# A two-layer transformer block on one core: norming, weight loads and a weight split moved from a stage's start into the stage before it

## The chip, the cores and the metric

The kernel runs on one core of a Trainium2 chip. The metric is the device time of one execution in microseconds (us). A core has TensorE (matrix products, with a queue of weight loads beside it), VectorE, ScalarE, GpSimd, and SyncE, which here only issues transfers. In rows they are PE, PEld, DVE, ACT, POOL and SP. Each engine runs its own instructions in order and waits for the others by semaphores.

## What is computed

A sequence of 2048 tokens of width 512 goes through four sublayers, each followed by a layernorm of the sum with its input. This case touches the seam between the first two.

```python
# differential attention: 16 head pairs, HD = 16, causal
aw = softmax(q @ k.T * HD**-0.5 + causal)                  # two maps per pair
aw = aw[:, :, 0] - lam * aw[:, :, 1]
attn = aw @ v                                              # 32 values per head
attn = attn * rsqrt(mean(attn * attn, -1) + 1e-5) * (1 - LAMBDA_INIT)   # norm per head
x = layernorm(x + attn @ Wo)
# mixture of experts: 8 experts, top 2, plus a low-rank part
scores = softmax(x @ G);  w = the two largest, kept
out = sum over e of w_e * (silu(x @ gate_e) * (x @ up_e)) @ down_e  +  low-rank (lora_A, lora_B)
x = layernorm(x + out)
# then a state-space layer (Mamba 2) and an int8 feed-forward
```

## The kernel before, in words

Tokens lie on the 128 partitions, in 16 tiles of 128 (`TT`). The program is a chain of blocks, each ended by a barrier of all engines: `qkv`, `attention`, `attend_out`, `experts`, `scan`, `finish`. Products are exact to float32: each operand is split in a high part (rounded, on ScalarE) and a low part (the rest, by subtraction, on VectorE or GpSimd), and `product3` adds three products. So each weight matrix is loaded raw, then split, before TensorE can use it.

**Attention** loops over 16 head pairs. A pair has 40 units (`units`): query chunk c of 512 tokens, key tile j of 128. Chunk 0 is units 0 to 3, chunk 1 is 4 to 11, chunk 2 is 12 to 23, chunk 3 is 24 to 39. For each unit TensorE writes scores (L440), ScalarE takes Exp of 2 x 512 of them (L510), and TensorE multiplies by V (L460). On the diagonal (the last four units of a chunk, 512, 384, 256 and 128 columns wide) GpSimd first zeroes the upper triangle (L368). TensorE writes the scores of unit u + 2 after Exp u and ahead of the product of unit u. When a chunk is full, ScalarE copies it (L537), TensorE turns it (L469), and VectorE's `combine` (L582 to L592) writes four tiles of `A`, one head's 32 columns. In all pairs but the last VectorE also reduces score maxima for later pairs; in the last it has only `combine`. Six times per pair, after units 15, 17, 26, 28, 30 and 32 (`SPLIT_AT`), ScalarE makes the high half of a later layer's weight (L517, L521), GpSimd the low half (L375), and SyncE stores both and loads the next.

**`attend_out`** has 21 slots, and in each every engine does steps for different tiles. The order is written by hand:
- TensorE in slot s: turn tile s of `A` (L718), turn tile s-3 of the result (L737), the router's and low-rank products of tile s-4 (`ao_pf`), the product with `Wo` of tile s-1 (`ao_po`).
- ScalarE: high part of `A` (`high_a`, L776), of the result (`high_x`, L780), a copy (L788), the root of a head norm (L770), squares (L766, 128x512), the layernorm's root (L784); behind slots 7, 11, 15 and 19 an Exp for four tiles' routing (L819).
- VectorE: scale tile s+1 of `A` by its head norms (L832, L834), low part `low_a` (L840), `low_x` (L844), sums of squares of tile s+2 (L825, L828), layernorm of tile s-2 (L864, L866), a copy (L870), then `add` of tile s-1: the sum with x (L854), its statistics (L856, L858) and variance (L860). Behind slots 7, 8, 11, 12 and so on come the routing steps of four tiles (L881 to L910).

SyncE loads `Wo`, `first` (low-rank and router weights), x, `gate`, and, when `Wo`'s raw copy is free, `up` in the same place. ScalarE and VectorE split `Wo` and `first`, ScalarE and GpSimd split `gate` (slot 0) and `up` (slot 2), 128x2048 each (L792, L708). The array `V_then_X` holds V in attention and the layer's result afterwards; the raw weights stand in its not yet written tiles.

## Time and profile before

| | us |
|---|---|
| median of three runs | 3621.58 (3617.08 to 3626.28) |
| the profiled execution | 3622.66 |
| its span | 3620.7 |
| TensorE busy | 3422.7 (95%) |
| VectorE busy | 2696.8 (74%) |
| ScalarE busy | 1947.7 (54%) |
| GpSimd busy | 918.3 (25%) |
| TensorE's granted clock, mean | 0.976 of full |

A row of a timeline has the start in us from the span's start, the duration, engine, line, operation, what is written from what, and in brackets how long the engine stood idle before it and what ended that. Lines are those of the kernel before. A row with x4 or x8 merges several instructions. The clock has two levels, 1.2 and 2.4 GHz. Attention ends at 1238 us, `attend_out` begins at 1239.1, `experts` at 1373.

### The profile page before, as it was taken

Reading aid. Unit: us, or ns where it says so; the run is one execution under the profiler, and the core shown is the slowest. Engines: PE = TensorE matmul, PEld = TensorE weight load, DVE = VectorE, ACT = ScalarE, POOL = GpSimd, SP = SyncE. Lnnn points to the kernel's source line nnn. Section 1 sums busy time; section 2 is a strip of 40 time slices with the busy share of each in tenths; the row PEclk is TensorE's granted clock in tenths of the full one; section 3 lists DMA queues with packets and bytes.
Section 4 is the critical chain, followed back from the end, with each engine's and each line's share of the span. In section 5 each row is a group of like instructions: output and inputs, shape, how many; then the busy total and the mean of one; then the engine's idle time right before and its main releaser. Section 6 shows DMA issues by size and latency. Waiting matters only on the chain. (4 is left out here: it accounts for less than half of the span.)

```text
span 3620.7 us, 58447 instructions
## 1 busy us (share of the span) xinstructions
PE 3422.7 (95%) x20912; PEld 2392.3 (66%) x20912; DVE 2696.8 (74%) x5252; ACT 1947.7 (54%) x2496; POOL 918.3 (25%) x821
## 2 busy tenths in 40 slices
PE   8889999999999788969999999999999999979998
PEld 6544444444444467756777777777777777758886
DVE  3577777777777384677999889998998889864444
ACT  3156656666667633434666566665666666543332
POOL 0022222222222200003443434443444444420000
PEclk9989999999999898989999999999999999989999
DMA  7443443443432211236555655565555555530100
GB/s 231 72 91 93 106 89 89 112 89 104 101 88 89 97 36 35 84 133 201 183 175 180 222 174 164 177 217 184 182 177 192 189 179 177 177 131 27 35 12 24
DMA packets 254975, 463.04 MB, mean 128 GB/s; under 512 B 48224, under 2 KB 62432, under 8 KB 251616
## 3 DMA queue, kind: packets, MB, share of 16 engines
q1 hardware_dynamic: 254688, 459.30, 41.6%
q8 instruction: 169, 2.77, 0.3%
q14 instruction: 118, 0.97, 0.1%
HBM read 363.49 MB, written 95.16 MB: 127 GB/s over the span
## 5 line engine op out<-in xcount | busy, mean ns | idle before, releaser
L510 ACT ACTIVATE probs<-prob_scores 128x1024 f32<-128x1024 f32 (+3 forms) x640 | 572.4, 896 | 381.0 <-PE prob_scores L440 373.1
L460 PE MATMUL times_v<-probs,VS 128*64 128x256 f32 (+2 forms) x4608 | 612.4, 382 | 14.2 <-ACT outT L537 13.0
L557 DVE TENSOR_REDUCE part_max<-ring 128x1 f32<-128x512 f32 x720 | 462.8, 685 | 115.3 <-PE ring L432 113.6
L49 PE MATMUL sc_pip<-sc_xh,sc_wl 128*128 128x512 f32 x1024 | 453.1, 443 | 18.6 <-DMA sc_xl<-x_low 14.0
L460 PEld LDWEIGHTS times_v<-probs,VS 128*64 128x64 f32 x4608 | 279.7, 136 | 253.7 <-issue 162.6
L1627 POOL TENSOR_TENSOR sc_xdd<-sc_xdt,sc_small 128x512 f32<-128x512 f32 x128 | 248.2, 1939 | 640.7 <-DVE sc_xdt L1849 640.7
L51 PE MATMUL sc_pip<-sc_xh,sc_wh 128*128 128x512 f32 x1024 | 405.8, 396 | 0.0
L50 PE MATMUL sc_pip<-sc_xl,sc_wh 128*128 128x512 f32 x1024 | 402.4, 393 | 0.0
L1840 DVE SCALAR_TENSOR_TENSOR sc_ca<-sc_xr,sc_chan,sc_ca 128x512 f32<-128x512 f32 x384 | 292.9, 763 | 13.6
L440 PE MATMUL prob_scores<-QS,KS 50*128 50x512 f32 (+3 forms) x1280 | 298.7, 463 | 1.6 <-ACT probs L510 1.6
L440 PEld LDWEIGHTS prob_scores<-QS,KS 50*128 50x128 f32 x1280 | 119.6, 184 | 214.2 <-ACT probs L510 121.0
L554 DVE CUSTOM_DVE_ANT_0 masked_scores<-ring,later_keys 128x128 f32<-128x128 f32 x480 | 216.2, 487 | 52.6 <-PE ring L432 49.5
L49 PEld LDWEIGHTS sc_pip<-sc_xh,sc_wl 128*128 128x128 f32 x1024 | 193.5, 189 | 91.2 <-issue 40.5
L432 PE MATMUL ring<-KS,QS 48*128 48x512 f32 (+3 forms) x1200 | 235.4, 388 | 12.8 <-DVE part_max L557 8.6
L1651 POOL TENSOR_TENSOR sc_ssq<-sc_ssq,sc_sq 128x512 f32<-128x512 f32 x112 | 181.1, 1617 | 252.2 <-ACT sc_sq L1802 252.2
L50 PEld LDWEIGHTS sc_pip<-sc_xl,sc_wh 128*128 128x128 f32 x1024 | 193.8, 189 | 69.4 <-issue 29.7
L1886 DVE TENSOR_TENSOR sc_gl<-sc_gx,sc_gh 128x512 fp32r<-128x512 f32 x128 | 223.2, 1744 | 0.0
L51 PEld LDWEIGHTS sc_pip<-sc_xh,sc_wh 128*128 128x128 f32 x1024 | 193.1, 189 | 42.1
L368 POOL TENSOR_SCALAR_AFFINE_SELECT probs<-probs 128x256 f32<-128x256 f32 x256 | 104.0, 406 | 456.8 <-ACT probs L510 456.8
L1691 PE MATMUL sc_py<-sc_M,sc_xdt 128*64 128x128 f32 x2048 | 207.4, 281 | 9.6 <-DVE sc_M L1860 9.6
L375 POOL TENSOR_TENSOR w_lo<-w_raw,w_hi 128x512 fp32r<-128x512 f32 x96 | 122.6, 1277 | 354.6 <-ACT w_hi L521 349.3
L49 PE MATMUL sc_pop<-sc_woh,sc_gl 128*128 128x512 f32 x512 | 204.9, 400 | 0.9 <-DVE sc_acc L1897 0.9
(333 smaller groups left out, 7215.2 us busy)
## 6 DMA issues: line engine op xcount, KB each, us to landing
sc_wh<-scan_W_high SPq DMA_DIRECT2D x256, 256.0 KB, 2.7
sc_wl<-scan_W_low SPq DMA_DIRECT2D x256, 256.0 KB, 3.0
sc_ce<-scan_expa SPq DMA_DIRECT2D x128, 512.0 KB, 5.2
sc_woh<-scan_Wo_high SPq DMA_DIRECT2D x128, 256.0 KB, 4.0
sc_wol<-scan_Wo_low SPq DMA_DIRECT2D x128, 256.0 KB, 4.6
w_raw<-in_Wg SPq DMA_DIRECT2D x64, 256.0 KB, 2.8
scan_W_high<-w_hi SPq DMA_DIRECT2D x64, 256.0 KB, 2.0
scan_W_low<-w_lo SPq DMA_DIRECT2D x64, 256.0 KB, 2.3
```

The source lines that it names most:

```text
L49: pe.matmul(out, ll, rh, start=start, stop=False)
L50: pe.matmul(out, lh, rl, start=False, stop=False)
L51: return pe.matmul(out, lh, rh, start=False, stop=stop)
L432: pe.matmul(slot(place["max", q, t, s])[:, 0:w], QS[q % NQK][rows, i * P:(i + 1) * P], KS[q % NQK][rows, c * CHUNK:c * CHUNK + w], start=T ...
L440: mm = pe.matmul(pb[u % 2][:, s, 0:w], KS[b][rows, j * P:(j + 1) * P], QS[b][rows, (c + 1) * CHUNK - w:(c + 1) * CHUNK], start=True, stop= ...
L460: mm = pe.matmul(po[MV * s:MV * (s + 1), CHUNK - w + n * h:CHUNK - w + (n + 1) * h], VS[p % 2][:, j, :], PT[u % NPT][:, s, n * h:(n + 1) * ...
L510: act.activation(PT[u % NPT][:, :, 0:w], pb[u % 2][:, :, 0:w], ACT.Exp).then_inc(exped, 1)
L554: dve.tensor_tensor_reduce(out=masked_out[:, s, 0:w], in0=slot(n)[:, 0:w], in1=later[:, CHUNK - w:], scale=1.0, scalar=NEG, op0=ALU.add, o ...
L557: dve.tensor_reduce(to, slot(n)[:, 0:w], AX.X, ALU.max).then_inc(emptied, 1)
L1627: pool.tensor_tensor(xdd[t % 2][:, :, :], xdt[t % 2][:, :, :], bc(t, 1), ALU.mult).then_inc(xdd_made, 1)
L1840: dve.scalar_tensor_tensor(out=to, in0=src, scalar=w, in1=to, op0=ALU.mult, op1=ALU.add).then_inc(conv if last else conv_step, 1)
L1886: dve.tensor_tensor(gl[t % 2][:, :, :], gx[:, :, :], gh[t % 2][:, :, :].bitcast(F32), ALU.subtract).then_inc(g_low, 1)
```

## The change

Three things move from `attend_out` into the last pair of attention.

1. The raw weights `Wo`, `first`, `up` and `gate` (3.4 MB) are loaded by SyncE once the last pair's V is staged, ahead of that pair's stores. `gate` and `up` have places of their own now, so the second load into `Wo`'s place falls away. `attend_out` waits for none of them.
2. `up` is split in the last pair in four pieces of 128x512: high halves on ScalarE behind Exp 19 to 22, the first waiting for all loads, low halves on GpSimd behind the four weight splits that follow unit 23's triangle.
3. Tiles 0 to 11 of `A` are squared and summed by VectorE behind the `combine` of chunks 0, 1 and 2, two tiles an operation; one step makes the mean squares of 12 tiles, ScalarE takes their root in one Sqrt behind unit 28's weight split, and VectorE takes the reciprocal and scales 12 tiles ahead of its last `combine`. `attend_out` squares, sums and scales only tiles 12 to 15 (`LATE`).

The array of mean squares is the same for both stages (`inv_rms`, before `ao_ms`).

```diff
@@ attention
+    UP_AT, ROOT_AT = (19, 20, 21, 22), 28
+    up_hi, up_lo = g.QS[1], g.KS[1]
+    NORMED = 4 * (NCH - 1)
@@ GpSimd, behind the low halves that follow a unit's triangle
+                        if p == PAIRS - 1 and u == ends[NCH - 2]:
+                            for n in range(len(UP_AT)):
+                                pool.wait_ge(up_high, n + 1)
+                                pool.tensor_tensor(up_lo[:, piece(n)], g.raw_up[:, piece(n)], up_hi[:, piece(n)].bitcast(F32), ALU.subtract).then_inc(up_low, 1)
@@ SyncE, ahead of the last pair's stores
+                sp.wait_ge(v_staged, PAIRS)
+                for to, src in next_w:
+                    sp.dma_start(to, src).then_inc(next_in, 16)
                 keep_weights(PAIRS - 1)
+                sp.wait_ge(next_in, 16 * len(next_w))
@@ ScalarE, behind exp and split_high of unit n
+                        if n // NU == PAIRS - 1 and n % NU in UP_AT:
+                            k = UP_AT.index(n % NU)
+                            if k == 0:
+                                act.wait_ge(next_in, 16 * len(next_w))
+                                act.wait_ge(scored, (PAIRS - 1) * NU)
+                            act.activation(up_hi[:, piece(k)], g.raw_up[:, piece(k)], ACT.Copy).then_inc(up_high, 1)
+                        if n == (PAIRS - 1) * NU + ROOT_AT:
+                            act.wait_ge(rms_ready, 1)
+                            act.activation(g.ms[:, 0:NORMED, :], g.ms[:, 0:NORMED, :], ACT.Sqrt).then_inc(rms_root, 1)
@@ VectorE
+                def sums(c):
+                    dve.wait_ge(out_done, (PAIRS - 1) * NCH + c + 1)
+                    for i in (4 * c, 4 * c + 2):
+                        if i:
+                            dve.wait_ge(summed, i // 2)
+                        rows = g.A[:, i:i + 2, :]
+                        dve.tensor_tensor(masked_out[:, :, :], rows, rows, ALU.mult).then_inc(squared, 1)
+                        dve.wait_ge(squared, i // 2 + 1)
+                        dve.tensor_reduce(g.ms[:, i:i + 2, :], masked_out[:, :, :].rearrange("p i (h d) -> p i h d", d=VD), AX.X, ALU.add).then_inc(summed, 1)
+                def scale_heads():
+                    c = 1.0 - LAMBDA_INIT
+                    ms = g.ms[:, 0:NORMED, :]
+                    dve.wait_ge(summed, NORMED // 2)
+                    dve.tensor_scalar(ms, ms, 1.0 / VD / c / c, LN_EPS / c / c, ALU.mult, ALU.add).then_inc(rms_ready, 1)
+                    dve.wait_ge(rms_root, 1)
+                    dve.reciprocal(ms, ms).then_inc(rms_inv, 1)
+                    dve.wait_ge(rms_inv, 1)
+                    for i in range(NORMED):
+                        rows = g.A[:, i, :].rearrange("p (h d) -> p h d", d=VD)
+                        dve.tensor_tensor(rows, rows, g.ms[:, i, :].unsqueeze(2).to_broadcast([P, PAIRS, VD]), ALU.mult).then_inc(scaled, 1)
@@ VectorE's loop
                         if u - 1 in ends:
                             combine(p, ends.index(u - 1))
+                            if p == PAIRS - 1:
+                                sums(ends.index(u - 1))
+                scale_heads()
                 combine(PAIRS - 1, NCH - 1)
@@ attend_out
+    LATE = TT - 4
@@ TensorE, turn_a
-                    pe.wait_ge(scaled, i + 1)
+                    if i >= LATE:
+                        pe.wait_ge(scaled, i - LATE + 1)
@@ ScalarE, ahead of the slots
-                square(0)
-                rms(0)
-                square(1)
-                weights_high(0, wo[0][:, :, :], raw_o)
-                rms(1)
-                square(2)
-                weights_high(1, wf[0][:, :, :], raw_f)
+                weights_high(wo[0][:, :, :], raw_o)
+                weights_high(wf[0][:, :, :], raw_f)
@@ VectorE
-                sums(0)
-                scale(0)
-                sums(1)
                 weights_low(0, wo[1][:, :, :], raw_o, wo[0][:, :, :])
                 for s in range(SLOTS):
-                    if s + 1 < TT:
+                    if LATE <= s + 1 < TT:
                         scale(s + 1)
@@
-                    if s + 2 < TT:
+                    if LATE <= s + 2 < TT:
                         sums(s + 2)
```

ScalarE in the last pair, from the copy of chunk 2 (`outT`) on. Before:

```order
L537 ACTIVATE outT<-times_v 128x512
L510 ACTIVATE probs<-prob_scores 128x1024
L517 ACTIVATE w_raw<-w_raw,w_norm 128x512
L521 ACTIVATE w_hi<-w_raw 128x512
L510 ACTIVATE probs<-prob_scores 128x1024 x2
L517 ACTIVATE w_raw<-w_raw,w_norm 128x512
L521 ACTIVATE w_hi<-w_raw 128x512
L510 ACTIVATE probs<-prob_scores 128x1024 x2
```

The same place now:

```order
L565 ACTIVATE outT<-times_v 128x512
L528 ACTIVATE probs<-prob_scores 128x1024
L535 ACTIVATE w_raw<-w_raw,w_norm 128x512
L539 ACTIVATE w_hi<-w_raw 128x512
L528 ACTIVATE probs<-prob_scores 128x1024 x2
L535 ACTIVATE w_raw<-w_raw,w_norm 128x512
L539 ACTIVATE w_hi<-w_raw 128x512
L560 ACT_TABLE_LOAD
L560 ACTIVATE inv_rms<-inv_rms 128x192
L528 ACT_TABLE_LOAD
L528 ACTIVATE probs<-prob_scores 128x1024 x2
```

Behind unit 28's split stand a table load, the Sqrt of 12 tiles' mean squares, and a second table load, ahead of Exp 29.

GpSimd at the end of attention, from the triangles of chunk 2 on. Before:

```order
L368 AFFINE_SELECT probs<-probs 128x2x128 x4
L375 TENSOR_TENSOR w_lo<-w_raw,w_hi 128x512 x4
L368 AFFINE_SELECT probs<-probs 128x2x128 x4
L346 UNCONDITIONAL_BRANCH
L2292 ISA
```

And now (`KS` is where `up`'s low half goes):

```order
L377 AFFINE_SELECT probs<-probs 128x2x128 x4
L384 TENSOR_TENSOR w_lo<-w_raw,w_hi 128x512 x4
L388 TENSOR_TENSOR KS<-V_then_X,QS 128x512 x4
L377 AFFINE_SELECT probs<-probs 128x2x128 x4
L355 UNCONDITIONAL_BRANCH
L2329 ISA
```

The four low halves of `up` come between the last weight split and the triangles of units 36 to 39.

VectorE at the start of `attend_out`. Before:

```order
L825 TENSOR_REDUCE ao_ms<-masked_scores 128x16
L828 TENSOR_SCALAR ao_ms<-ao_ms 128x16
L832 RECIPROCAL ao_ms<-ao_ms 128x16
L834 TENSOR_TENSOR A<-A,ao_ms 128x512
L825 TENSOR_REDUCE ao_ms<-masked_scores 128x16
L828 TENSOR_SCALAR ao_ms<-ao_ms 128x16
L874 TENSOR_TENSOR ao_wo_low<-V_then_X,ao_wo_high 128x2048
L832 RECIPROCAL ao_ms<-ao_ms 128x16
L834 TENSOR_TENSOR A<-A,ao_ms 128x512
L840 TENSOR_TENSOR ao_al<-ao_pa,ao_ah 128x512
```

And now:

```order
L914 TENSOR_TENSOR ao_wo_low<-V_then_X,ao_wo_high 128x2048
L880 TENSOR_TENSOR ao_al<-ao_pa,ao_ah 128x512
L914 TENSOR_TENSOR ao_wf_low<-V_then_X,ao_wf_high 128x544
L880 TENSOR_TENSOR ao_al<-ao_pa,ao_ah 128x512
L894 TENSOR_TENSOR V_then_X<-ao_po,later_keys 128x512
```

The low half of `Wo` is the stage's first work on VectorE, and the low part of tile 0 (`ao_al`) follows it directly.

## Rows read from the trace of the kernel before

**Rows 1.** Busy time by stretch, `attend_out`: us, then engines' busy time, clock, DMA
```profile
core 0: us, PE busy (x) PEld busy (x) DVE busy (x) ACT busy (x) POOL busy (x), PEclk, DMA share, GB/s
...
1272.40:1293.80 21.40, 20.92 (x132) 17.74 (x130) 20.53 (x53) 8.32 (x24) 0.00 (x0) 1.00 0.18 50
```

**Rows 2.** DMA issues at the stage's start: size, us to landing
```profile
V_then_X<-in_Wo SPq DMA_DIRECT2D x1, 1024.0 KB, 5.5
```

**Rows 3.** Timeline of the stage's start: start us, us, engine, line; idle before
```profile
1244.67 1.91 ACT L792 ACTIVATE ao_wo_high<-V_then_X 128x2048 fp32r<-128x2048 f32 x1 [2.84 <-DMA V_then_X<-in_Wo]
...
1250.62 0.77 PE L49 MATMUL ao_po<-ao_wo_high,ao_al 128*128 128x512 f32 x1
...
1254.73 0.60 PE L718 MATMUL ao_pa<-ident,A 128*128 128x128 f32 x4
...
1255.61 2.88 DVE L828 TENSOR_SCALAR ao_ms<-ao_ms 128x16 f32<-128x16 f32 x1
...
1260.05 0.15 DVE L860 TENSOR_SCALAR ao_rx<-row_stats 128x1 f32<-128x1 f32 x1
```

**Rows 4.** Timeline of VectorE, one slot of the stage
```profile
1288.45 0.15 DVE L860 TENSOR_SCALAR ao_rx<-row_stats 128x1 f32<-128x1 f32 x1
...
1289.40 0.68 DVE L840 TENSOR_TENSOR ao_al<-ao_pa,ao_ah 128x512 fp32r<-128x512 f32 x1
...
1290.60 0.68 DVE L825 TENSOR_REDUCE ao_ms<-masked_scores 128x16 f32<-128x512 f32 x1
...
1291.40 0.16 DVE L864 RECIPROCAL ao_rx<-ao_rx 128x1 f32<-128x1 f32 x1
...
1293.79 0.15 DVE L860 TENSOR_SCALAR ao_rx<-row_stats 128x1 f32<-128x1 f32 x1
```

**Rows 5.** Timeline of VectorE, two adds in the stage's tail
```profile
1343.61 0.69 DVE L854 TENSOR_TENSOR V_then_X<-ao_po,ao_x 128x512 f32<-128x512 f32 x1 [1.83 <-PE ao_po L51]
...
1348.55 0.69 DVE L854 TENSOR_TENSOR V_then_X<-ao_po,later_keys 128x512 f32<-128x512 f32 x1 [0.34 <-PE ao_po L51]
```

**Rows 6.** Timeline of the stage: clock falls, table load, slots with routing
```profile
1261.15 1.11 PE L718 MATMUL ao_pa<-ident,A 128*128 128x128 f32 x4 [3.07 <-DVE A L834]
...
1270.91 0.66 PE L737 MATMUL ao_px<-ident,V_then_X 128*128 128x128 f32 x4 [2.11 <-DVE V_then_X L866]
...
1294.20 1.28 ACT L819 ACT_TABLE_LOAD   x1
...
1295.49 0.23 ACT L819 ACTIVATE ao_ex<-ao_ex 128x32 f32<-128x32 f32 x1
...
1308.03 1.11 PE L737 MATMUL ao_px<-ident,V_then_X 128*128 128x128 f32 x4 [1.99 <-DVE V_then_X L866]
...
1309.62 0.15 DVE L860 TENSOR_SCALAR ao_rx<-row_stats 128x1 f32<-128x1 f32 x1
...
1317.65 0.15 DVE L860 TENSOR_SCALAR ao_rx<-row_stats 128x1 f32<-128x1 f32 x1
```

**Rows 7.** Timeline of attention's last pair, units 26 to 36
```profile
1216.68 0.87 DVE L592 TENSOR_TENSOR A<-out 128x128 f32<-128x128 f32 x1
...
1219.79 1.92 ACT L510 ACTIVATE probs<-prob_scores 128x1024 f32<-128x1024 f32 x2
...
1221.38 0.50 PE L440 MATMUL prob_scores<-QS,KS 50*128 50x512 f32 x2
...
1227.08 1.26 POOL L375 TENSOR_TENSOR w_lo<-w_raw,w_hi 128x512 fp32r<-128x512 f32 x1 [2.75 <-ACT w_hi L521]
...
1231.05 0.41 POOL L368 TENSOR_SCALAR_AFFINE_SELECT probs<-probs 128x256 f32<-128x256 f32 x1 [2.70 <-ACT probs L510]
...
1232.55 1.08 PE L460 MATMUL times_v<-probs,VS 128*64 128x256 f32 x8
```

**Rows 8.** VectorE's groups by shape, whole run: xcount, busy us, mean ns
```profile
L1860 DVE TENSOR_TENSOR sc_M<-sc_M,sc_CB 128x1024 f32<-128x1024 f32 x128 | 156.5, 1223 | 1.1 <-ACT sc_M L1777 1.1
...
L1352 DVE RECIPROCAL A<-A 128x256 f32<-128x256 f32 x4 | 7.0, 1753 | 0.1
```

More of the change, by code:

```diff
@@ L235, in _, with attention @@
                                       g.KS[0][rows, c * CHUNK:c * CHUNK + w], start=True, stop=True).then_inc(filled, 1)
-def attention(nc, g, QD, KD, lams, scan_w):
+def attention(nc, g, QD, KD, lams, scan_w, next_w):
     PARTS = 3 * HD
@@ L331, in attention @@
         out_inv, out_weight, out_weighed, out_done = (g.sem("out_" + n) for n in ("inv", "weight", "weighed", "done"))
+        next_in, up_high, up_low = g.sem("next_weights_in"), g.sem("up_high"), g.sem("up_low")
+        squared, summed, rms_ready, rms_root, rms_inv, scaled = (
+            g.sem("at_" + n) for n in ("squared", "summed", "rms_ready", "rms_root", "rms_inv", "scaled"))
+        piece = lambda n: slice(n * CHUNK, (n + 1) * CHUNK)
         loads = lambda q: 16 * 12 * (q // NQK + (q % NQK > 1))
@@ L631, with attend_out @@
 AR = LR + EX
-def attend_out(nc, g, x_dram, A, X, xh, xl, lr, w, Wo, first, gate, up, mv):
+def attend_out(nc, g, x_dram, A, X, xh, xl, lr, w, raw, mv):
     SLOTS = TT + 5
+    LATE = TT - 4
+    raw_o, raw_f, raw_g = raw
     NB = TT // 4
@@ L661, in attend_out @@
         sem = lambda name: g.sem("ao_" + name)
-        w_in, w_high, w_low, w_rest = [sem(f"w_in{n}") for n in range(4)], sem("w_high"), sem("w_low"), sem("w_rest")
+        w_high, w_low, w_rest = sem("w_high"), sem("w_low"), sem("w_rest")
         x_in = [sem(f"x_in{b}") for b in range(2)]
@@ L687, in load_x @@
                     sp.dma_start(xin[i % 2][:, :], x_dram[i * P:(i + 1) * P, :]).then_inc(x_in[i % 2], 16)
-                sp.dma_start(raw_o, by_row(Wo)).then_inc(w_in[0], 16)
-                sp.dma_start(raw_f, by_row(first)).then_inc(w_in[1], 16)
-                for i in range(2):
-                    load_x(i)
-                sp.dma_start(raw_g, by_row(gate)).then_inc(w_in[2], 16)
-                sp.wait_ge(w_low, 1)
-                sp.dma_start(raw_o, by_row(up)).then_inc(w_in[3], 16)
-                for i in range(2, TT):
-                    sp.wait_ge(added, i - 1)
+                for i in range(TT):
+                    if i >= 2:
+                        sp.wait_ge(added, i - 1)
                     load_x(i)
@@ L705, in _ @@
                                    pattern=[[1, EX], [-1, EX]], channel_multiplier=0).then_inc(made, 1)
-                for n, (raw, (hi, lo)) in enumerate(((raw_g, wg), (raw_o, wu))):
-                    pool.wait_ge(w_high, 3 + n)
-                    pool.tensor_tensor(lo[:, :], flat(raw), hi[:, :].bitcast(F32), ALU.subtract).then_inc(w_rest, 1)
-                pool.wait_ge(w_rest, 2)
+                pool.wait_ge(w_high, 3)
+                pool.tensor_tensor(wg[1][:, :], flat(raw_g), wg[0][:, :].bitcast(F32), ALU.subtract).then_inc(w_rest, 1)
+                pool.wait_ge(w_rest, 1)
             @block.tensor
@@ L788, in keep_l, with weights_high @@
                     act.activation(lr[:, i, :], pf[i % 2][:, 0:LR], ACT.Copy).then_inc(read_l, 1)
[L790 to L791 removed]
+                def weights_high(hi, raw):
                     act.activation(hi, raw, ACT.Copy).then_inc(w_high, 1)
[L794 to L800 removed]
+                weights_high(wo[0][:, :, :], raw_o)
+                weights_high(wf[0][:, :, :], raw_f)
                 for s in range(SLOTS):
@@ L923, in _ @@
                         low_x(s - 3)
-                    if s + 2 < TT:
+                    if LATE <= s + 2 < TT:
                         sums(s + 2)
@@ L2329, in two_layers @@
                 qkv(nc, g, xT, Wq, Wk, Wv, QD, KD)
-            with nc.sbuf_tensor("A", [P, TT, E], F32) as g.A:
-                attention(nc, g, QD, KD, (lq1, lk1, lq2, lk2), (Wg, WoT, norm_table, D["W"], D["Wo"]))
+            with nc.sbuf_tensor("A", [P, TT, E], F32) as g.A, nc.sbuf_tensor("inv_rms", [P, TT, PAIRS], F32) as g.ms:
+                raw_f = X[:, 6:8, :].rearrange("p a n -> p (a n)")[:, 0:EK * AR].rearrange("p (k n) -> p k n", k=EK)
+                raw_o, raw_g, g.raw_up = X[:, 8:12, :], X[:, 2:6, :], X[:, 12:16, :].rearrange("p k n -> p (k n)")
+                attention(nc, g, QD, KD, (lq1, lk1, lq2, lk2), (Wg, WoT, norm_table, D["W"], D["Wo"]),
+                          ((raw_o, by_row(Wo)), (raw_f, by_row(first)), (X[:, 12:16, :], by_row(up)), (raw_g, by_row(gate))))
                 g.end_stage()
@@ L2336, in two_layers @@
                     lr = g.A[:, 0:4, :].rearrange("p a (b n) -> p (a b) n", n=LR)
-                    attend_out(nc, g, x, g.A, X, xh, xl, lr, w, Wo, first, gate, up, mv)
+                    attend_out(nc, g, x, g.A, X, xh, xl, lr, w, (raw_o, raw_f, raw_g), mv)
                     experts(nc, g, X, xh, xl, lr, w, g.A[:, 4:, :].rearrange("p a n -> p (a n)"), (down, lora_b, scan_first),
```

35 lines of the change are left out of this document (15 added, 20 removed).

## The prediction

> **What bounds the kernel now.** The edit touches two neighbouring places: attention's last pair (to 1238 us) and the stage behind it, `attend_out` (1239 to 1373 us). I read the windows of that stage first. In its even stretch [rows 1] TensorE is busy 20.9 of 21.4 us and VectorE 20.5: both are nearly full, so work taken from VectorE gives back only the distance to TensorE's own limit. Hence I followed one token tile from slot to slot. A tile's last row on VectorE is L860, the variance of its layernorm; from one L860 to the next is one slot, and the time table below is made of these rows. Then I read the stage's start, where everything waits for `Wo`'s transfer [rows 2, 3], and the last pair unit by unit, because the new waits and instructions go there.
>
> **The stage, slot by slot.** (a) *Start.* `Wo` takes 5.5 us from issue to landing [rows 2], and ScalarE splits it at 1244.67 [rows 3]. Now it is in place, so the split begins with the stage, at 1239.2: 5.5 earlier. VectorE's half starts 1.95 later and takes 2.29; `low_a(0)` comes right behind it, at 1243.3, with no reciprocal and scale of a tile between; the first product starts 0.9 later, 1244.2 against 1250.62. Before, the product took 4.1 (1250.62 to 1254.73, the transposes behind it), its first matmuls slow. I take 4.4, since TensorE rests ahead of it now. VectorE's add follows at 1248.7. Before, the add also stood behind L828, 2.88 us for 16 elements per row while GpSimd split 128x2048 [rows 3]; no L828 comes before tile 12 now. From the add to L860 it is 1.66 (0.71, 0.73 and 0.22 from start to start): tile 0 at 1250.3 against 1260.05, 9.7 earlier.
>
> (b) *One even slot* takes 5.34 before (1288.45 to 1293.79 [rows 4]). The sums (L825, L828) go, and L864 starts where L825 did: 0.80 less. The scale (L832, L834) goes too, but brings nothing: `low_a` (L840) starts 0.95 after L860, and the other way to it, ScalarE's root and `high_a`, takes as long. The scale only covered a wait. VectorE's chain becomes 4.54. TensorE's own slot is longer: in the stage's tail, where VectorE waits for it, its products end 4.94 apart [rows 5]. So an even slot becomes 4.94, a gain of 0.40, not the 1.7 of the removed work. In the first slots tiles of later steps are missing: 4.54 without `low_x` and the copy is 3.9, without the copy 4.45, and tile 3 meets TensorE, 4.75. Tiles 1 to 3: 1254.2, 1258.6, 1263.4. Three times 4.94: tile 6 at 1278.2, before 1293.79.
>
> (c) *Slots with routing.* Tiles 6 to 8 took 15.83 before (1293.79 to 1309.62 [rows 4, 6]): an Exp with its table load (1.28), then the routing steps. VectorE's chain sets these slots, and from it go the sums twice (1.60) and, behind the routing, one scale that hid nothing (0.89): 13.34 are left, tile 8 is at 1291.5, 18.1 earlier.
>
> (d) *The clock behind the routing.* Before, TensorE waited for a scale and then 1.99 for a norm, fell to 1.2 GHz (the 4 transposes at 1308.03 take 1.11), and tile 9 came 8.03 after tile 8 [rows 6]. Now one wait is left, for tile 7's norm, of 2.25 by the same table. An idle of 2.11 left the clock up at 1270.91, one of 3.07 had it down at 1261.15 [rows 6]; 2.25 is nearer to the first. Then tile 9 follows after 5.34 (it has sums again: tiles 12 to 15 are still normed here), 2.7 less. From there on nothing differs. **The stage ends 18.1 + 2.7 = 20.8 us earlier**; if the clock falls, 18.1.
>
> **What the last pair pays.** (e) *Four high halves of `up`* on ScalarE, 0.6 each (1.91 for 128x2048 [rows 3]), after units 19 to 22. Units 21 to 23 have 384, 256 and 128 columns of scores per half, so ScalarE, late by one piece at most, catches up: 0. The transfers (3.4 MB) are issued at the pair's start, some 25 us before they are wanted; end to end at 5.5 per MB [rows 2] they need 18.7: 0. Squares and sums of chunks 0 and 1 lie in VectorE's idle time: 0.
>
> (f) *The root at unit 28.* ScalarE is free for it at 1219.79, where Exp 29 starts before [rows 7]. VectorE ends `combine` of chunk 2 at 1217.55 (L592), and only then squares and sums tiles 8 to 11: two products of 128x1024 at 1.22 [rows 8] and two reductions of the same count, for which 0.68 at 512 [rows 4] gives 1.21: 4 x 1.25 = 5.0. The product reads two operands in SBUF, as L592 does, and L592 took 0.87 for 128 elements beside a split on GpSimd; one product meets such a split: 1.1 at most. With L828's successor, 0.3, the mean squares are ready at 1224.0 (1222.9 without the meeting). Sqrt 0.35, then the table load back to Exp, 1.28 [rows 6] (the load for Sqrt lies inside the wait): Exp 29 starts at 1225.7, **5.9 late**. Queued behind the root are Exp 29 to 39 and two weight splits; TensorE's scores of unit 31 (1221.38 [rows 7]) wait for Exp 29, with 0.6 of slack: 5.3 late. TensorE idles over 5 us by then, so as at 1261.15 it goes on at 1.2 GHz. Such a fall cost 2.7 at tile 9 and 1.2 in the stage's first product; I take 2.0. Unit 36's product, 1232.55 before, could start at 1239.8.
>
> (g) *Four low halves on GpSimd* stand behind its last weight split and ahead of the four triangular selects of units 36 to 39. That split was at 1227.08 [rows 7] and is now some 5.7 late, 1232.8. Five operations of 1.25 end at 1239.0, plus 0.6 to 1.2 for meeting VectorE's 12 scales, plus the select, 0.41 (1231.05 [rows 7]): unit 36 can start at 1240.3, half a us behind (f). So (f) and (g) nearly hide each other; alone, (g) would cost 1.1. VectorE's reciprocal of 192 (1.35, between 1.75 at 256 [rows 8] and the small ones) and 12 scales at 0.6 end by 1236, before its last `combine`: 0. **The last pair ends 8 us later**, between 5.5 (early mean squares, short fall of the clock) and 10.
>
> **The sum.** -20.8 + 8.0 = -12.8. The profiled execution took 3622.66 (span 3620.7), the median of three runs 3621.58. So 3609.9 on its own time and **3608.8** on the median, 0.35% faster.
>
> On the meeting of VectorE and GpSimd: the Trainium skill (SBUF — State Buffer, Who interferes with whom) says that a VectorE operation with two SBUF inputs and a GpSimd one that reads SBUF exclude each other for a whole instruction, whoever comes first. The trace agrees (L592, 0.87). By that rule the 12 scales in a row could hold GpSimd off longer than (g) has it, by another 1.2 or so.
>
> **Rivals.**
> *No stall at the root.* If the mean squares were there in time, the pair would pay two loads and the root (2.9 less 0.6) and little of (g): +2.5, sum -18.3, **3603.3**. Against it: the sums can't begin before 1217.55 and need 5 us, where ScalarE leaves 2.2. 0.14.
> *The stage gives less.* The clock falls at tile 9 (2.7), and GpSimd's split of `gate`, wanted at 1244.0, gets ahead of VectorE's `ao_wf_low`, wanted at 1243.9, and holds it 4.6 us, of which 1.3 reach the chain: sum -8.8, **3612.8**. Both are close calls. 0.25.
> *A table switch costs more than its load.* In the trace an Exp starts 0.01 behind its load's end (1294.20, 1.28, 1295.49 [rows 6]), which speaks against it; if each of the two added switches cost its load twice, 2.6: **3611.4**. 0.05.
> The Trainium skill (ScalarE: Activation LUTs, What ACT_TABLE_LOAD costs) gives a drain of 1.38 us with each switch; an estimate by it is this same rival.
> *Slower: the raw weights come late.* ScalarE's first high half, behind Exp 19, waits for all four transfers, and Exp 20 to 39 stand behind it. Each us beyond the 25 adds one. To lose over 11 us in all they must come 24 us late, that is take near 50 us where I bound them by 18.7: 3634. 0.03.
> *That the change doesn't do what it says*: the order of instructions shows all its parts; no chance kept.
>
> **How the numbers follow.** Forecast 0.53 (3605.5 to 3613), rivals 0.14, 0.25, 0.05, 0.03. A measurement of this kernel can tell about 0.3% (10.9 us) from no change; the line is 3610.7. Of the forecast's 0.53 some 0.42 lies below it, with the stall-free rival: faster 0.56. Same: 0.11 + 0.25 + 0.05 = 0.41. Slower: 0.03. Range 3602 to 3617, which takes in the first two rivals and their bounds.
>
> **What would show it.** Right: ScalarE idle 3 to 4.5 us before a Sqrt of 128x192, and TensorE over 5 before unit 31's scores; four splits of 128x512 back to back on GpSimd with the selects behind them; the first `ao_po` product 5 to 6.5 us after the stage's start; slots of 4.94 with VectorE waiting for TensorE; tile 9's L860 5.3 behind tile 8's. Wrong: even slots still of 5.3, or of 4.5; a clock of 1.2 GHz in the middle of the stage; a last pair that ends under 5 or over 10 us later; any difference before the last pair or behind the stage.

## The result: 0.34% faster, and the profile after

The changed kernel takes 3608.81 us, the median of six executions (3607.37 to 3617.26), beside 3622.86 of the kernel before (six, 3617.08 to 3626.28). The ratio is 0.9966, 95% interval 0.9953 to 0.9979. That is a gain of 12.3 us by the ratio and 14.0 by the medians. The forecast was 3608.8.

The profiled execution is the longest of the six, 3617.26 with a span of 3615.5. I therefore compare by stretches. The **pair stretch** runs from unit 24's product in the last pair to `attend_out`'s first instruction. The **stage** runs from there to the first weight load of `experts`.

| us | pair stretch | stage | sum against before |
|---|---|---|---|
| before | 25.15 (1214.01 to 1239.16) | 133.9 (to 1373.0) | |
| after | 32.91 (1219.89 to 1252.80) | 115.9 (to 1368.7) | +7.8 - 18.0 = -10.2 |
| after, second profile (`after_again`) | 33.82 | 114.7 | +8.7 - 19.2 = -10.5 |

ScalarE at the root in the last pair of the changed kernel (L539 makes a weight's high half, L560 is the Sqrt, L528 the Exp; columns as in [rows 3]):

```profile
1225.14 0.63 ACT L539 ACTIVATE w_hi<-w_raw 128x512 fp32r<-128x512 f32 x1
1225.79 1.28 ACT L560 ACT_TABLE_LOAD   x1
1229.78 0.36 ACT L560 ACTIVATE inv_rms<-inv_rms 128x192 f32<-128x192 f32 x1 [2.71 <-DVE inv_rms L637]
1230.16 1.28 ACT L528 ACT_TABLE_LOAD   x1
1231.45 1.94 ACT L528 ACTIVATE probs<-prob_scores 128x1024 f32<-128x1024 f32 x2
```

VectorE, the squares (L629), sums (L631) and scales (L643) of the same stretch:

```profile
1223.47 1.23 DVE L629 TENSOR_TENSOR masked_scores<-A 128x1024 f32<-128x1024 f32 x1
...
1225.99 2.21 DVE L629 TENSOR_TENSOR masked_scores<-A 128x1024 f32<-128x1024 f32 x1
1228.23 1.22 DVE L631 TENSOR_REDUCE inv_rms<-masked_scores 128x32 f32<-128x1024 f32 x1
1229.49 0.26 DVE L637 TENSOR_SCALAR inv_rms<-inv_rms 128x192 f32<-128x192 f32 x1
...
1231.56 10.55 DVE L643 TENSOR_TENSOR A<-A,inv_rms 128x512 f32<-128x512 f32 x12
```

TensorE behind it: unit 31's scores (L458) after the wait, products (L478) at half clock, one in which the clock rises, and unit 36's product at 1246.13:

```profile
1232.53 0.79 PE L458 MATMUL prob_scores<-QS,KS 50*128 50x512 f32 x2 [5.19 <-ACT probs L528]
1233.26 1.97 PE L478 MATMUL times_v<-probs,VS 128*64 128x256 f32 x8
...
1238.51 1.58 PE L478 MATMUL times_v<-probs,VS 128*64 128x256 f32 x8
...
1246.13 1.08 PE L478 MATMUL times_v<-probs,VS 128*64 128x256 f32 x8
```

ScalarE idles between its table load and the Sqrt until VectorE has the mean squares. TensorE then waits 5.19 us and works at 1.2 GHz for 6 to 7 us: a product takes 1.97 instead of 1.08. Up to unit 24 the pair loses nothing: it begins 5.91 behind the kernel before (copy of V at 1182.50 against 1176.59), and unit 24's scores are 5.88 behind (1216.68 against 1210.80). So the loads and the high halves of `up` cost nothing.

In the stage, the two adds (L894), the variance (L900) and `low_a` (L880) on VectorE in one even slot answer to [rows 4]. `turn_x` on TensorE at tile 9 answers to the clock fall in [rows 6]:

```profile
1286.36 0.69 DVE L894 TENSOR_TENSOR V_then_X<-ao_po,ao_x 128x512 f32<-128x512 f32 x1 [0.37 <-PE ao_po L51]
1288.03 0.15 DVE L900 TENSOR_SCALAR ao_rx<-row_stats 128x1 f32<-128x1 f32 x1
1288.94 0.69 DVE L880 TENSOR_TENSOR ao_al<-ao_pa,ao_ah 128x512 fp32r<-128x512 f32 x1 [0.76 <-ACT ao_ah L822]
...
1291.33 0.69 DVE L894 TENSOR_TENSOR V_then_X<-ao_po,later_keys 128x512 f32<-128x512 f32 x1 [0.38 <-PE ao_po L51]
1293.00 0.15 DVE L900 TENSOR_SCALAR ao_rx<-row_stats 128x1 f32<-128x1 f32 x1
```

```profile
1304.76 0.66 PE L783 MATMUL ao_px<-ident,V_then_X 128*128 128x128 f32 x4 [2.12 <-DVE V_then_X L906]
```

From variance to variance (start to start of two L900 rows) it is 4.97 now, and VectorE has two waits in each slot: 0.76 for ScalarE's high part, 0.37 for TensorE's product. Windows of the changed kernel (columns as in [rows 1]) confirm it: the last row, full clock and TensorE busy throughout, answers to [rows 1].

```profile
1252.80:1368.70 115.90, 91.58 (x512) 78.29 (x513) 82.44 (x210) 40.36 (x88) 5.52 (x4) 0.86 0.13 37
1273.00:1293.00 20.00, 20.00 (x132) 17.81 (x130) 14.92 (x37) 5.38 (x16) 0.00 (x0) 1.00 0.19 54
```

### The profile page after: what moved, and what is told of

The parts are those of the page before. It is cut to its first block and busy times, and to the rows that moved or that the text cites. A ratio compares the mean times of both kernels' runs of the same rounds, so it can differ in the third digit from the quotient of the medians.

```text
span 3615.5 us, 58404 instructions
## 1 busy us (share of the span) xinstructions
PE 3425.9 (95%) x20912; PEld 2392.2 (66%) x20912; DVE 2700.5 (75%) x5230; ACT 1943.3 (54%) x2478; POOL 921.3 (25%) x824
## 5 line engine op out<-in xcount | busy, mean ns | idle before, releaser
L528 ACT ACTIVATE probs<-prob_scores 128x1024 f32<-128x1024 f32 (+3 forms) x640 | 573.2, 897 | 386.0 <-PE prob_scores L458 377.6
L478 PE MATMUL times_v<-probs,VS 128*64 128x256 f32 (+2 forms) x4608 | 617.4, 384 | 14.1 <-ACT outT L565 12.9
L478 PEld LDWEIGHTS times_v<-probs,VS 128*64 128x64 f32 x4608 | 281.3, 137 | 257.2 <-issue 166.5
L458 PE MATMUL prob_scores<-QS,KS 50*128 50x512 f32 (+3 forms) x1280 | 301.0, 467 | 6.0 <-ACT probs L528 6.0
L458 PEld LDWEIGHTS prob_scores<-QS,KS 50*128 50x128 f32 x1280 | 120.3, 185 | 220.5 <-ACT probs L528 125.6
L450 PE MATMUL ring<-KS,QS 48*128 48x512 f32 (+3 forms) x1200 | 236.4, 390 | 12.8 <-DVE part_max L585 8.6
L1728 PE MATMUL sc_py<-sc_M,sc_xdt 128*64 128x128 f32 x2048 | 207.2, 281 | 10.2 <-DVE sc_M L1897 10.2
```

The source lines that it names most:

```text
L450: pe.matmul(slot(place["max", q, t, s])[:, 0:w], QS[q % NQK][rows, i * P:(i + 1) * P], KS[q % NQK][rows, c * CHUNK:c * CHUNK + w], start=T ...
L458: mm = pe.matmul(pb[u % 2][:, s, 0:w], KS[b][rows, j * P:(j + 1) * P], QS[b][rows, (c + 1) * CHUNK - w:(c + 1) * CHUNK], start=True, stop= ...
L478: mm = pe.matmul(po[MV * s:MV * (s + 1), CHUNK - w + n * h:CHUNK - w + (n + 1) * h], VS[p % 2][:, j, :], PT[u % NPT][:, s, n * h:(n + 1) * ...
L528: act.activation(PT[u % NPT][:, :, 0:w], pb[u % 2][:, :, 0:w], ACT.Exp).then_inc(exped, 1)
```

## The experiments

Line numbers in rows are each kernel's own. Diffs are against the changed kernel unless said otherwise, and the ratio in each is to the kernel before on the same chip.

**1. The norming alone.** Loads and splits of the weights stay in `attend_out`.

```diff
-                sp.wait_ge(v_staged, PAIRS)
-                for to, src in next_w:
-                    sp.dma_start(to, src).then_inc(next_in, 16)
@@ and the high and low halves of up in attention; attend_out loads and splits as before
```

> Only the norming of tiles 0 to 11 is moved; the weights are loaded and split in attend_out as before. My theory: the root's stall is there in full without the weights: from the product of unit 24 to attend_out's first instruction 31.5 to 32.9 us, TensorE idle 5.2 ahead of the scores of unit 31. The stage's start waits 5.5 for Wo's transfer (first product 9 to 11 us behind the start), even slots 4.94 to 4.97, tile 9 at 5.3 or 6.4; the stage is 10 to 14 us shorter and the kernel 3613 to 3620: by itself this part brings 3 to 7. The rival, that GpSimd's four low halves set the longer last pair: the stretch is 29 or less.

Measured: 3616.0, ratio 0.9983 (0.9974 to 0.9992). Pair stretch 33.90 (+8.8), over my range. The stall is the same (Sqrt after 2.71 idle, TensorE 5.19). Low halves of `up` can't be the cause, they aren't there. What differs from the changed kernel is the time at half clock: three products at 1.97 and one in which the clock rises (1.45), there two and one.

```profile
1226.71 0.80 PE L449 MATMUL prob_scores<-QS,KS 50*128 50x512 f32 x2 [5.19 <-ACT probs L519]
...
1232.69 1.97 PE L469 MATMUL times_v<-probs,VS 128*64 128x256 f32 x8
1234.59 0.79 PE L449 MATMUL prob_scores<-QS,KS 50*128 50x512 f32 x2
1235.32 1.45 PE L469 MATMUL times_v<-probs,VS 128*64 128x256 f32 x8
```

Stage 121.9 (-12.0), its first product 10.6 behind the start, since ScalarE idles 9.00 until `Wo` has landed. Together -3.2 in the touched stretches, while the ratio says -6.2.

**2. The weights alone.** All 16 tiles are normed in `attend_out`.

```diff
-    LATE = TT - 4
+    LATE = 0
-                            if p == PAIRS - 1:
-                                sums(ends.index(u - 1))
-                scale_heads()
@@ and the root in attention; squares, roots and scales of tiles 0 and 1 ahead of the slots, as before
```

> Only the loads and the split of up lie in the last pair; all 16 tiles are squared, summed and scaled in attend_out as before. My theory: no root in the last pair, so no stall; from the product of unit 24 to attend_out's first instruction 25.2 to 26.3 us (before 25.15, the change 32.91): only the four low halves of up can hold a select, by 1.1 at most. At the stage's start Wo's split begins at once; a Sqrt's table load and tile 0's norm lie beside it; the first product 2.5 to 5.5 us earlier than before, and one VectorE wait behind a GpSimd split of 128x2048 less. Even slots stay at 5.34 and tile 9 at 8 us. The stage is 5 to 8 us shorter, the kernel 3614 to 3618. The rival, that the transfers or the splits of up burden the last pair (SyncE's queue, ScalarE late for units 23 to 28): the stretch is over 27 us.

Measured: 3618.67, 0.9987 (0.9978 to 0.9997), just over my range. Pair stretch 26.56 (+1.4), 0.3 over it; the expected (g) stands in its rows, an idle of 1.06 ahead of unit 36's product, which waits for GpSimd's queue:

```profile
1229.81 4.97 POOL L388 TENSOR_TENSOR KS<-V_then_X,QS 128x512 fp32r<-128x512 f32 x4
1234.73 1.13 POOL L377 TENSOR_SCALAR_AFFINE_SELECT probs<-probs 128x256 f32<-128x256 f32 x3
```

```profile
1235.19 1.08 PE L478 MATMUL times_v<-probs,VS 128*64 128x256 f32 x8 [1.06 <-POOL probs L377]
```

Stage 129.7 (-4.2, where I expected -5 to -8; tile 0's norm and one wait of 2.87 behind GpSimd's split stay, and the first product took 5.1 where it took 4.1 before). Together -2.8, while the ratio says -4.7.

At the stage's start the two halves need each other: its first product starts 11.5 behind the stage's start in the kernel before, 10.6 and 8.5 with one half, 4.9 with both. The start waits for whichever is still there, the weights or the norm. In the touched stretches the halves are worth 3.2 and 2.8, and both together 10.2 to 10.5; of the difference of 4.2 to 4.5, the stage has 1.8 to 3.0, and the pair the rest, where (g) is hidden behind the root and the clock differs from profile to profile. The whole times don't show that both are worth more than their sum: by the ratios the halves gain 6.2 and 4.7, together 10.9, and the change 12.3 and 10.9.

**3. Eight tiles instead of twelve in attention.**

```diff
-    NORMED = 4 * (NCH - 1)
+    NORMED = 8
-                            if p == PAIRS - 1:
+                            if p == PAIRS - 1 and u < 20:
-    LATE = TT - 4
+    LATE = 8
```

> The changed kernel with tiles 0 to 7 instead of 0 to 11 normed in the last pair: their sums are done long before unit 28, so the root finds them ready. My theory (the stall is the wait for chunk 2's sums): ScalarE does load, Sqrt, load without idling, 2.9 us; Exp 29 is 2.9 later than in the kernel before, TensorE idles 2.3 ahead of the scores of unit 31 and stays at 2.4 GHz; the stretch is 27.3 to 28.3 us (the change 32.91). The stage: tiles 0 to 5 as in the change (4.94 a slot), from tile 6 on as before: 14 to 15 us shorter than before. The kernel 3609 to 3613: what the pair saves, the stage loses. The rival, that the two table switches or the scales cost the time and not the wait: 31 us or more.

Measured: 3611.85, 0.9969 (0.9957 to 0.9980). ScalarE runs load, Sqrt, load without a pause:

```profile
1224.38 1.28 ACT L560 ACT_TABLE_LOAD   x1
1225.67 0.31 ACT L560 ACTIVATE inv_rms<-inv_rms 128x128 f32<-128x128 f32 x1
1226.00 1.28 ACT L528 ACT_TABLE_LOAD   x1
1227.29 1.94 ACT L528 ACTIVATE probs<-prob_scores 128x1024 f32<-128x1024 f32 x2
```

TensorE waits 2.44 (expected 2.3), and 0.8 goes to a short fall of the clock that I had not expected. Pair stretch 28.51 (+3.4), 0.2 over my range, stage 118.9 (-15.0). Unit 31's scores are 2.5 late where the changed kernel has 5.27: the root with its two loads costs 2.5, and waiting for chunk 2's sums 2.75, just the larger part. The total is as good as the changed kernel's: what the pair saves, the stage loses.

**4. GpSimd's low halves of `up` 12 units earlier**, ahead of the triangles of chunk 2.

```diff
+                        if p == PAIRS - 1 and u == ends[NCH - 2]:
+                            for n in range(len(UP_AT)):
+                                pool.wait_ge(up_high, n + 1)
+                                pool.tensor_tensor(...)
                         for n in range(by_unit.get(u, 0)):
@@ the same block removed behind this loop
```

> The changed kernel with GpSimd's four low halves of up moved ahead of the four weight splits behind unit 23's triangle. I measure the stretch from unit 24's product with V to the first instruction of attend_out: 25.1 us in the kernel before, 32.9 in the changed one. Theory (root stall and GpSimd queue hide each other; the stall of ScalarE at the root with the lower clock behind it sets the end): 32.4 to 32.9, the time within 1 us of the changed kernel's. Rival (GpSimd's queue ahead of unit 36 sets the end): 27 to 30, 3 to 6 us faster than the changed kernel. The four low halves should take 4 x 1.25 = 5.0 us there instead of 5.87.

Measured: 3611.3, 0.9965 (0.9953 to 0.9977), pair stretch 31.31. It is shorter than in the changed kernel, but the 1.6 is the clock again: the second product behind the stall takes 1.24, not 1.97. The root's stall is there in full (5.20). The stretch is under my range and over the rival's. With the stage (117.2) the touched stretches give -10.5, as in the changed kernel, so GpSimd's queue costs that kernel nothing that shows. The four low halves took 4.96 in their new place, as expected.

**5. The same, with the root behind unit 32 instead of 28.**

```diff
-    UP_AT, ROOT_AT = (19, 20, 21, 22), 28
+    UP_AT, ROOT_AT = (19, 20, 21, 22), 32
@@ and the edit of experiment 4
```

> As low_early, and ScalarE's root of the mean squares behind unit 32's weight split instead of unit 28's. The mean squares are then ready before ScalarE comes to them, so only the root and two table loads (2.9 us) remain on ScalarE, with a shorter idle of TensorE. Theory: the stretch shrinks from 32.9 to 28 to 30 us, 3 to 5 us less than the changed kernel; no idle of ScalarE ahead of the Sqrt. Rival (the wait is not what costs; the transfers or the late scales of VectorE set the end): 32 to 33.

Measured: 3609.02, 0.9963 (0.9950 to 0.9977), pair stretch 31.55: the stretch is a miss. The Sqrt waits for nothing, but unit 32's weight arrives late, and a split, two table loads and the Sqrt stand behind it ahead of Exp 33. The rows of ScalarE and TensorE:

```profile
1227.87 0.72 ACT L535 ACTIVATE w_raw<-w_raw,w_norm 128x512 f32<-128x512 f32 x1 [1.59 <-DMA w_raw<-in_WoT]
```

```profile
1233.32 0.80 PE L458 MATMUL prob_scores<-QS,KS 50*128 50x512 f32 x2 [4.60 <-ACT probs L528]
1234.05 1.98 PE L478 MATMUL times_v<-probs,VS 128*64 128x256 f32 x8
```

TensorE idles 4.60 all the same (0.73 at this place before), its scores are 3.9 late, and 2.5 more goes to the clock. Of the 3.9, 3.1 are the root and its two loads, all of it felt since no slack is left behind this split, and 0.8 is the weight, which lands that much later than before; why it does, no run shows. Stage 114.8, together -12.7.

**6. The root behind the last Exp**, low halves as in 4, and the scales of tiles 0 to 11 in `attend_out`'s slots.

```diff
-                        if n == (PAIRS - 1) * NU + ROOT_AT:
+                        if n == PAIRS * NU - 1:
-                    for i in range(NORMED): ... dve.tensor_tensor(rows, rows, g.ms ...)
+                scale(0)
+                scale(1)
                 weights_low(0, wo[1][:, :, :], raw_o, wo[0][:, :, :])
                 for s in range(SLOTS):
+                    if s + 2 < LATE:
+                        scale(s + 2)
@@ and the edit of experiment 4; TensorE's turn_a waits for every tile's scale again
```

> As low_early, and ScalarE takes the root behind the last Exp of attention, VectorE only the reciprocal there; the scales of tiles 0 to 11 go back into attend_out, two ahead of the slots and one in each slot. Theory: the last pair pays about 0.6 us (Sqrt's table load ahead of the last copy), stretch 25.5 to 26.5; the scales in the slots are free, since low_a there waits 0.95 us behind L900's row for ScalarE anyway, except behind the routing (0.6) and at the start: even slots stay 4.94 to 4.97. In all 6 to 7.5 us faster than the changed kernel, some 3602. Rival (VectorE's work counts in the slots): even slots of 5.5, and 4 us of that gain lost again.

Measured: 3605.1, 0.9951 (0.9939 to 0.9964). Pair stretch 25.53 (+0.4), as expected; stage 117.1 (-16.8), together -16.4. That is 5.9 to 6.2 better than the changed kernel in these stretches; the ratios say 5.4 and 6.9 (expected 6 to 7.5), and the intervals overlap, so the gain is shown by the rows and not by the times. ScalarE at the end of the pair (L560 is the root, L565 the copy ahead of the last `combine`):

```profile
1235.24 1.28 ACT L560 ACT_TABLE_LOAD   x1
1236.53 0.36 ACT L560 ACTIVATE inv_rms<-inv_rms 128x192 f32<-128x192 f32 x1
1236.80 0.58 ACT L565 ACTIVATE outT<-times_v 128x512 f32<-128x512 f32 x1
```

The scales come back into the slots and cost nothing there: the first six intervals are 3.84 to 4.97, as in the changed kernel; 0.6 at the start and 0.6 behind the routing are their price. No second table load is needed. At the start VectorE's low half of `first` runs into GpSimd's split of `gate` (4.59 instead of 0.71), and nobody is late: the first product takes 5.3 at 1.2 GHz anyway.

**7. and 8. What sets a slot.** Both are edits of the kernel before. `slot_no_scale` leaves out the reciprocals and scales of tiles 3 to 11; `slot_no_sums` leaves out their squares, sums and roots (the same guard in `square`, `rms` and `sums`). Each was executed once, so I compare slots only.

```diff
                 def scale(i):
+                    if 3 <= i < 12:
+                        return
```

> The kernel before, with the scale by head norms (reciprocal and product, L832 and L834) left out for tiles 3 to 11; sums and roots stay. Theory: the scale covers a wait of low_a for ScalarE, so even slots (L860 to L860, tiles 2 to 6) stay at 5.3 us and VectorE shows an idle of some 0.8 ahead of low_a; only behind the routing of slot 8 is 0.9 saved, and tile 9 comes sooner since TensorE waits less there. Rival (work removed from VectorE comes off): even slots of 4.94, TensorE's own.

> The kernel before without squares, sums and roots for tiles 3 to 11 (their scale takes the reciprocal of another tile's mean square; this part of the computation is left out). My theory: the even slots fall from 5.34 to 4.94 to 4.97, where TensorE is the bound, and VectorE's add is behind a wait of 0.3 to 0.4 for TensorE's product. The rival, that VectorE is the only bound: 4.54, all 0.80 of the sums.

Measured: 5.29 to 5.31 a slot without the scales (5.34 before), and VectorE waits 0.76 for ScalarE's high part where the scale stood. Without the sums a slot takes 4.96 to 4.99 (tiles 4 to 6; TensorE worked at 1.2 GHz at tile 3, which took 8.97), and VectorE's add waits for TensorE. One row of each:

```profile
1278.38 0.69 DVE L843 TENSOR_TENSOR ao_al<-ao_pa,ao_ah 128x512 fp32r<-128x512 f32 x1 [0.76 <-ACT ao_ah L777]
```

```profile
1284.21 0.69 DVE L861 TENSOR_TENSOR V_then_X<-ao_po,later_keys 128x512 f32<-128x512 f32 x1 [0.36 <-PE ao_po L51]
```

The scale covered a wait, and TensorE is the bound at 4.94. Behind the routing, where the scale covered nothing, tile 8 came 8.11 behind tile 7 without it (8.99 before), as expected, and tile 9 5.30 behind tile 8.

**9. The changed kernel again**, for a second profile.

> The changed kernel a second time, with a profile of its own. In its first profile pair 0 of attention, which the change does not touch, took 77.99 us (73.07 in the kernel before) because TensorE's clock stayed at 1.2 GHz longer. My theory: that is chance between executions; pair 0 is 73 to 74 here and the profiled execution at 3607 to 3611. The root's stall must come again as it was: TensorE idle 5.2 ahead of the scores of unit 31, 5.27 late against the kernel before; only the time at 1.2 GHz behind it may differ (2.4 us over the 5.27 in the first profile, 0.8 to 3.4 in other kernels with the same stall), so the stretch from unit 24's product to attend_out is 31 to 34. Even slots 4.94 to 4.97 again. The rival, that the change itself burdens attention's first pair: 78 again.

Measured: 3610.88, 0.9970 (0.9958 to 0.9982), profiled execution 3609.82. Pair 0 of attention takes 73.04 (77.99 in the first profile, 73.07 before). The windows show why the first profile was some 5 us longer; row one is the changed kernel, row two its second profile:

```profile
200.00:210.00 10.00, 10.00 (x45) 4.33 (x42) 4.93 (x12) 4.05 (x5) 0.41 (x1) 0.50 0.47 53
```

```profile
200.00:210.00 10.00, 9.82 (x66) 4.83 (x66) 7.63 (x20) 5.59 (x7) 0.41 (x1) 0.90 0.36 41
```

The stall is the same (2.72 and 5.20), the time at half clock is longer, as in experiment 1: pair stretch 33.82, inside what I expected. At tile 9 TensorE's clock falls in this profile, though its wait is as long as in the first (2.10 and 2.12), and it falls only when 1.8 us of work are done: the transposes take 0.66 as at full clock, and the product with `Wo` behind them has 0.63 a step, as at 1.2 GHz.

```profile
1299.36 0.66 PE L783 MATMUL ao_px<-ident,V_then_X 128*128 128x128 f32 x4 [2.10 <-DVE V_then_X L906]
...
1301.71 0.63 PE L50 MATMUL ao_po<-ao_wo_low,ao_ah 128*128 128x512 f32 x1
```

**10. TensorE kept at work while it waits for `Wo`.** On experiment 6: transposes of the identity whose results nobody uses, and `low_a(0)` ahead of `scale(2)`.

```diff
+                def warm(n):
+                    for k in range(n):
+                        pe.transpose(px[1][:, k % EK, :], g.ident[:, :], g.ident[:, :])
+                warm(4)
                 for s in range(SLOTS):
                     if s < TT:
                         turn_a(s)
+                    if s == 1:
+                        warm(9)
```

> The kernel with the root behind the last Exp, with two more edits at attend_out's start: low_a(0) ahead of scale(2), and 4 + 9 transposes of the identity on TensorE (results unused) around the first turns of A, where it else waits for the split of Wo. My theory: the first product starts 4.9 us behind the stage's start instead of 5.5, and tile 0's variance comes 12.1 behind it instead of 12.73. If the transposes keep TensorE's clock up or bring it up earlier, the product takes 3.0 to 4.4 instead of 5.3 and tile 0 is at 10 to 11.2. Stage 114.5 to 116.5 (117.1), the kernel 3602 to 3605, same as without them within the measurement. The rival, that the transposes do nothing for the clock or come in the way of the product: product 5.3 again, tile 0 at 12.1 or later.

Measured: 3606.99, 0.9953 (0.9940 to 0.9967). The first product runs at full clock, 2.9 instead of 5.3, but tile 0 comes 13.2 behind the start and the stage takes 120.4. VectorE's low half of `first` is caught by GpSimd's split, and now the product no longer hides it: TensorE waits 3.35 for the next `low_a` and falls to 1.2 GHz. This makes 2.3 of the 3.4 by which the stage is longer than in experiment 6; tile 9, at half clock here and not there, adds 2.5, and tile 13 gives 1.5 back. Pair stretch 26.25, together -12.3.

```profile
1248.64 5.09 DVE L917 TENSOR_TENSOR ao_wf_low<-V_then_X,ao_wf_high 128x544 fp32r<-128x544 f32 x1
```

```profile
1254.99 0.80 PE L49 MATMUL ao_po<-ao_wo_high,ao_al 128*128 128x512 f32 x1 [3.35 <-DVE ao_al L883]
```

**11. The same with GpSimd's split behind that low half, in four pieces.**

```diff
+                pool.wait_ge(w_low, 2)
+                for n in range(4):
+                    of = slice(n * E, (n + 1) * E)
+                    pool.tensor_tensor(wg[1][:, of], flat(raw_g)[:, of], ...).then_inc(w_rest, 1)
```

> root_end_warm with GpSimd's low half of gate behind VectorE's low half of first, in four pieces of 128x512 instead of one of 128x2048. In root_end_warm the first product ran at 2.4 GHz from its start (2.9 us instead of 5.3), but VectorE's 0.72 for the low half of first took 5.09 beside the split of gate, low_a(1) and the add stood behind it, TensorE waited 3.35 and the second product ran at 1.2 GHz: tile 0 13.2 behind the start, tile 1 another 5.7. My theory: now no VectorE operation is held longer than one piece (1.3); the low half of first takes 0.72, TensorE waits under 2 ahead of the second product and keeps its clock; tile 0 is 10 to 10.6 behind the stage's start, tile 1 3.8 to 4.5 behind it, the stage 113 to 115 and the kernel 3600 to 3605. The rival, that the pieces hold VectorE as long as the one split did: tile 0 at 12 or later, and nothing is won.

Measured: 3604.52, 0.9945 (0.9931 to 0.9958). Tile 0 is 9.86 behind the start, tile 1 another 4.01. The low half takes its 0.72, the four pieces 5.79 beside VectorE's work. Pair stretch 25.86, stage 115.3 (0.3 over my range, with tile 9 at half clock again, 7.75), together -17.8. It is the best of all in the middle, though its interval overlaps with those of 6 and 10, and a little with the changed kernel's (0.9953 to 0.9979).

## Why the prediction was right

The sum was -12.8, made of -20.8 and +8.0. The touched stretches gave -10.2 and -10.5 in the two profiles, and the ratios (0.9966, 0.9970) say -12.3 and -10.9. So 3608.8 was met more closely than its terms were: the 14.0 between the medians is more than the touched stretches gave. The rest lies where nothing was changed, and there the profiles scatter: from `experts` on, 2242 to 2249 us. That forecast and median agree to 0.1 us is luck; the pair's term was right (+7.8 and +8.7 for +8.0), and the stage's was 2.8 and 1.6 too large. In the first profile 1.0 of that is the first product, 1.6 tile 13 and 0.2 tile 3; in the second 1.1 is tile 9, and the rest small pieces. All but 0.2 and 0.5 of it is the clock.

*Stage, (a) start: right but for the clock.* The first product starts 4.9 behind the stage's start (forecast 5.0), and no L828 stall is left. The product took 5.3, wholly at 1.2 GHz, where I had 4.4, and tile 0 comes 12.1 behind the start, forecast 11.1; in the second profile the clock rose within the product, which took 4.5, and tile 0 comes 11.3 behind the start.

*(b) Even slots: right.* 4.94 to 4.97, forecast 4.94, and 3.83 and 4.44 in the first two (3.9, 4.45). The third was 4.94, not 4.75. Experiments 7 and 8 show both halves of the argument by themselves: the scale was cover, the sums were not.

*(c) Routing: right.* 6.05 and 7.30, as worked out.

*(d) Tile 9: right once, by luck.* The idle was 2.12 (forecast 2.25) and the clock stayed up, 5.30. In the second profile an idle of 2.10 was followed by a fall and 6.45, and so were the 2.10 and 2.11 of experiments 1, 4 and 5. I had judged by the length of the idle, and that does not decide it: 2.71 to 2.72 at the same place left the clock up in experiment 6 and had it down in 10 and 11. What decides it, no run shows. Nor is the price fixed: the fall costs 1.15 here (6.45 less 5.30), where it began only 1.8 us behind the wait, and 2.5 in experiments 10 and 11 against 6, where the clock was down right behind it; I had 2.7. Tile 13, on which the forecast was silent, has the same: 8.06 here and 6.47 there.

*(e) Loads and high halves of `up`: right*, nothing, as shown with the result.

*(f) The root: right.* VectorE's mean squares lag as summed: Sqrt at 1229.78, where 1224.0 on the clock of the kernel before becomes 1229.9 with this profile's offset of 5.88. One square meets GpSimd's split (2.21 instead of 1.23). Unit 31's scores are 5.27 late against [rows 7], forecast 5.3. The clock cost 2.4 (unit 36's product 7.70 late less 5.27), forecast 2.0; the same stall gave 0.8, 3.4 and 3.3 in experiments 4, 1 and 9, so that the 2.0 was met within a scatter as large as itself.

*(g) The low halves: right.* Alone 1.06 of idle (experiment 2), beside (f) 0.09: GpSimd's queue was done at 1245.7, 1.2 behind Exp 36, but TensorE itself came to unit 36's product only at 1246.04, and started it at 1246.13. In the second profile it was held by nothing. The 12 scales took 10.55 in place of 7.3 (experiment 5, without a split on GpSimd beside them), with GpSimd's splits stretched to 1.5 to 1.7 and the four low halves to 5.87, and all but the 0.09 stayed hidden. On the last point the Trainium skill (SBUF — State Buffer, Who interferes with whom) had warned of such an exclusion; the trace agrees, and here it costs next to nothing, while in experiment 10 TensorE waited 3.35 for it.

*The rivals and the signs.* "No stall" was kept away by the 2.71 of idle ahead of the Sqrt. The sign asked for 3 to 4.5; with the table load of 1.28 that lies inside the wait it is 4.0. "The stage gives less" did half come: the clock fell at tile 9 in one profile and not in the other, for 1.15. A clock of 1.2 GHz in the stage and a difference ahead of the last pair were signs of being wrong; both were seen, and experiment 9 shows the second (pair 0) to be chance. The race of `ao_wf_low` was won by 0.06 us (1257.56 against 1257.62), and experiment 6, which lost it, shows that my price of 1.3 was wrong there: nothing, so long as the product is slow. "A table switch costs more than its load" is out: Exp 29 starts 0.01 behind the load, and the two loads and the Sqrt of experiment 3 follow each other within 0.02. So the drain of 1.38 per switch that the Trainium skill gives (ScalarE: Activation LUTs, What ACT_TABLE_LOAD costs) is not seen here. The raw weights were issued at 1183, and the slowest landed 10.4 after its issue, well ahead of ScalarE's first high half at 1211.89.

Of the experiments' forecasts, number 5 failed, for the reasons named there, and 10 in part. The pair stretches of 1, 2, 3 and 4 lay 0.2 to 1.1 outside their ranges, mostly by the clock, and 2 promised more of the stage than it gave. Number 6 shows what the change had left: the root need not stand in the middle of a pair whose Exp needs the other table.

## What to carry to other kernels

Work moved off a stage's start into the stage before pays only if everything that the start waits for moves with it; here the stage's first product came 0.8 and 3.0 us sooner with one half, and 6.6 with both. Put a step that needs another function table or a late sum where its engine's queue ends, not in the middle of it: the root behind the last Exp lengthens the pair by 0.4 us, where behind unit 28 it took 6 to 9 in four profiles, and what its place saves is clear in the rows, not yet in the whole times. And removed work on a full engine is worth only the distance to the next engine's limit, here 0.4 of 1.7 us a slot.
